# The FFN and scan stage of a decoder kernel: tile product behind a chunk's first scan, statistics and normalisation by rows, features in halves, another order of the first loads, the last state summed by TensorE

## The reference

```python
x = x + L0_ffn(layernorm(x), lut, gate_idx, up_idx, down_idx)
# gate = xn @ lut[gate_idx].T ; up = xn @ lut[up_idx].T          (1376 columns each)
# out  = (silu(gate) * up) @ lut[down_idx].T

def step(state, xs):                    # 512 channels x 16 states, 512 steps, 4 sequences
    dA = jnp.exp(d_t[..., None] * A)
    state = state * dA + (d_t * u_t)[..., None] * B_t[:, None, :]
    y_t = jnp.einsum('ben,bn->be', state, C_t)
```

## Time and profile before

| | us |
|---|---|
| median of 3 runs (lowest to highest) | 2331.14 (2330.18 to 2335.35) |
| the profiled execution's own time | 2330.81 |
| its span from first to last instruction | 2329.0 |
| PE busy | 2123.0 (91%) |
| DVE busy | 1740.6 (75%) |
| POOL busy | 1064.9 (46%) |
| ACT busy | 955.4 (41%) |

### The profile page before, as it was taken

One profiled execution on the slowest core, in us unless ns is written; L12 is line 12 of the kernel. 1 busy time (PEld: TensorE's weight loads), 2 busy tenths in 40 slices (PEclk: granted clock), 3 DMA queues, 4 the chain that ended last, 5 costly groups with the idle time before them and its releaser, 6 DMA issues. The chain is left out here.

```text
span 2329.0 us, 25406 instructions
## 1 busy us (share of the span) xinstructions
PE 2123.0 (91%) x7538; PEld 1145.1 (49%) x7538; DVE 1740.6 (75%) x2988; ACT 955.4 (41%) x1827; POOL 1064.9 (46%) x811
## 2 busy tenths in 40 slices
PE   6999999999999998996899998999699999999858
PEld 3555555455545553444646556465354545455334
DVE  3888788978888877886888888889646474665554
ACT  2433334334334335664646546466224232332321
POOL 3553433334435512233899898999631011010143
PEclk9999999999999999998999999999789999999979
DMA  7000000000000011656535526453264243432121
GB/s 272 24 19 19 19 23 23 16 26 19 18 19 23 19 49 63 225 220 243 206 135 190 194 91 207 141 202 110 82 198 118 73 116 94 108 109 69 50 113 54
DMA packets 100377, 232.73 MB, mean 100 GB/s; under 512 B 16542, under 2 KB 33824, under 8 KB 97844
## 3 DMA queue, kind: packets, MB, share of 16 engines
q1 hardware_dynamic: 86504, 183.71, 24.4%
q10 hardware_dynamic: 13260, 47.73, 6.0%
q0 software_dynamic: 512, 0.13, 0.0%
HBM read 158.89 MB, written 46.27 MB: 88 GB/s over the span
## 5 line engine op out<-in xcount | busy, mean ns | idle before, releaser
L1583 POOL TENSOR_TENSOR s_state<-s_b_rows,s_delta_u 128x1024 f32<-128x1024 f32 x128 | 303.4, 2383 | 37.6 <-DMA s_b_rows<-scan_bc 35.2
L1627 DVE TENSOR_TENSOR_SCAN s_state<-s_decay,s_state 128x512 f32<-128x512 f32 x256 | 305.0, 1212 | 13.5 <-ACT s_decay L1569 11.0
L908 POOL TENSOR_SCALAR a_prob<-a_prob,a_rsum 128x256 f32<-128x256 f32 x256 | 143.4, 579 | 373.1 <-DVE a_rsum L781 373.0
L1742 PE MATMUL c_bank<-c_xn_parts,c_w_parts 128*128 128x512 f32 (+1 forms) x1056 | 275.8, 412 | 6.5 <-DMA c_w_parts<-ffn_weights_lo 6.4
L1569 ACT ACTIVATE s_decay<-s_delta,s_a 128x512 f32<-128x512 f32 x256 | 173.5, 689 | 229.3 <-DVE s_state L1627 223.5
L1742 PEld LDWEIGHTS c_bank<-c_xn_parts,c_w_parts 128*128 128x128 f32 (+1 forms) x1056 | 201.0, 191 | 68.7 <-issue 21.0
L433 DVE TENSOR_SCALAR f_picks<-f_mask,f_lut_xor,f_lut 128x260 int32<-128x260 int32 x512 | 228.5, 519 | 7.6 <-DVE f_mask L424 0.6
L580 PE MATMUL a_bank<-a_xn_t,a_wq_then_context 128*128 128x512 f32 x512 | 224.3, 592 | 0.0
L641 PE MATMUL a_bank<-a_wo,a_out_t 128*128 128x512 f32 x512 | 222.3, 592 | 0.0
L2257 ACT ACTIVATE d_prob_t<-d_score 128x512 f32<-128x512 f32 x256 | 139.0, 596 | 175.0 <-PE d_score L2124 174.1
L443 DVE COPY_PREDICATED f_picks<-f_mask,f_picks 128x260 int32<-128x260 int32 x448 | 193.6, 491 | 21.1
(11 more groups left out here) (224 smaller groups left out, 3738.0 us busy)
## 6 DMA issues: line engine op xcount, KB each, us to landing
s_b_rows<-scan_bc SPq DMA_DIRECT2D x64, 512.0 KB, 3.8
c_w_parts<-ffn_weights_hi ACTq DMA_DIRECT2D x39, 512.0 KB, 3.7
c_w_parts<-ffn_weights_lo ACTq DMA_DIRECT2D x39, 512.0 KB, 4.9
d_unit<-diff_parts SPq DMA_DIRECT2D x26, 512.0 KB, 3.8
f_idx<-in_idx SPq DMA_DIRECT2D x64, 130.0 KB, 2.2
ffn_weights<-f_picks SPq DMA_DIRECT2D x64, 130.0 KB, 1.7
d_qs<-d_hi SPq DMA_DIRECT2D x128, 64.0 KB, 2.0
d_factor<-in_factors SPq DMA_DIRECT2D x16, 512.0 KB, 3.6
```

Source lines behind the costliest of these rows:

```text
L1583: pool.tensor_tensor(self.state[:, s], row.broadcast_to([P, 2, T]), self.delta_u[:, h % 2], ALU.mult) \
L1627: dve.tensor_tensor_scan(self.state[:, s, e, :], self.decay[u % 2][:], self.state[:, s, e, :], 0.0, ALU.mult, ALU.add).then_inc(self.scann ...
L1742: mm = nc.tensor.matmul(banks[b][0:width[o], :], w_parts[:, n % SLOTS, w, at:at + width[o]], xn_parts[:, x_, k, :], start=((k, w, x_) == t ...
```

## The change

- `lift` and the statistics and normalisation of the next pass move behind the first scan of the chunk and ahead of the weighing (`beside`). The statistics are made one row tile at a time at pieces 4 to 7, their moments at piece 8, and the normalised rows are written one at a time at pieces 12 to 15.
- The features at piece 28 are taken in two halves, two ahead of the chunk's second scan and two behind it.
- At the start of the stage ACT loads weight tile 0 (before: tile 1), and SP loads weight tile 1 behind the first pair of B rows (before: tile 0, ahead of delta, delta_u and the rows).
- At the end the last chunk is weighed ahead of the last `add`, POOL no longer adds it to its group, and PE adds it to y itself; DVE takes each half of y as soon as it is ready.

```diff
--- before.py
+++ after.py
@@ -1465,6 +1465,7 @@
         self.weighed = core.sem("s_weighed")
         self.gathered = core.sem("s_gathered")
         self.summed = core.sem("s_summed")
+        self.last_summed = core.sem("s_last_summed")
         self.y_taken = core.sem("s_y_taken")
 
     def sync_setup(self, sp):
@@ -1500,11 +1501,13 @@
         sp.dma_start(self.scratch["y"][h // 2, :, h % 2 * 2:h % 2 * 2 + 2, :], self.y[:]) \
             .then_inc(self.stored, 16)
 
-    def sync(self, sp):
+    def sync(self, sp, behind_first_row):
         self.load_half(sp, 0)
         for h in range(2 * B):
             for r in range(8 * h, 8 * h + 8):
                 self.load_rows(sp, r)
+                if r == 0:
+                    behind_first_row()
                 if r == 8 * h + 4:
                     if h:
                         self.store_half(sp, h - 1)
@@ -1536,6 +1539,17 @@
                                        start=(g % 4 == 0), stop=(g % 4 == 3))
         mm.then_inc(self.summed, 1)
 
+    def sum_last(self, pe):
+        g, c = self.GROUPS - 1, self.N - 1
+        pe.wait_ge(self.gathered, 3 * g + 2)
+        for e in range(2):
+            self.nc.tensor.matmul(self.y_bank[e][:], self.consts.ident[:], self.group[:, g % 2, e, :],
+                                  start=False, stop=False)
+        pe.wait_ge(self.weighed, c + 1)
+        for e in range(2):
+            self.nc.tensor.matmul(self.y_bank[e][:], self.consts.ident[:], self.state[:, c % self.SLOTS, e, :],
+                                  start=False, stop=True).then_inc(self.last_summed, 1)
+
     def tensor_setup(self, pe):
         self.spread_c(pe, 0)
 
@@ -1546,7 +1560,7 @@
             self.sum_group(pe, (c - 6) // 4)
 
     def tensor_end(self, pe):
-        self.sum_group(pe, self.GROUPS - 1)
+        self.sum_last(pe)
 
     def scalar_setup(self, act):
         act.wait_ge(self.a_in, 16)
@@ -1607,8 +1621,7 @@
             self.feed(pool, c + 2)
 
     def gpsimd_end(self, pool):
-        for c in (self.N - 2, self.N - 1):
-            self.gather(pool, c)
+        self.gather(pool, self.N - 2)
 
     def vector_setup(self, dve):
         dve.wait_ge(self.a_step, 1)
@@ -1637,15 +1650,20 @@
 
     def take_y(self, dve, h):
         dve.wait_ge(self.y_in, (h + 1) * 16)
-        dve.wait_ge(self.summed, 4 * h + 4)
+        if h < 2 * B - 1:
+            dve.wait_ge(self.summed, 4 * h + 4)
         for e in range(2):
+            if h == 2 * B - 1:
+                dve.wait_ge(self.last_summed, e + 1)
             dve.tensor_tensor(self.y[:, e, :], self.y_bank[e][:], self.y[:, e, :], ALU.add) \
                 .then_inc(self.y_taken, 1)
 
-    def vector(self, dve, c):
+    def vector(self, dve, c, behind_scan, behind_weighing):
         self.scan(dve, c, 0)
+        behind_scan()
         if c:
             self.weigh(dve, c - 1)
+        behind_weighing()
         self.scan(dve, c, 1)
         if c % 16 == 3 and c > 16:
             self.take_y(dve, c // 16 - 1)
@@ -1708,8 +1726,7 @@
         @block.sync
         def _(sp):
             scan.sync_setup(sp)
-            load_weights(sp, 0, 0)
-            scan.sync(sp)
+            scan.sync(sp, lambda: load_weights(sp, 0, 1))
             scan.sync_end(sp)
 
         @block.tensor
@@ -1793,7 +1810,7 @@
                         act.wait_ge(full[1], fill_turn(i, o) + 1)
                     load_weights(act, *divmod(n, OT))
 
-            load_ahead(1)
+            load_ahead(0)
             features(0)
             scan.scalar_setup(act)
             for n in range(2, SLOTS):
@@ -1814,8 +1831,8 @@
 
         @block.vector
         def _(dve):
-            def features(i):
-                for k in range(KD):
+            def features(i, tiles=range(KD)):
+                for k in tiles:
                     dve.wait_ge(xn_rounded, i * KD + k + 1)
                     nc.vector.tensor_tensor(xn_parts[:, 1, k, :], banks[k % 2][:], xn_parts[:, 0, k, :].bitcast(F32),
                                             ALU.subtract).then_inc(free[k % 2], 1)
@@ -1830,6 +1847,39 @@
                 dve.wait_ge(full[tt % 2], down_turn(i, tt) + 1)
                 nc.vector.tensor_tensor(x[:, i, tt, :], banks[tt % 2][:], x[:, i, tt, :], ALU.add) \
                     .then_inc(free[tt % 2], 1)
+
+            def stats_row(i, tt):
+                row = nc.vector.bn_stats(norm.stats[:, tt, :], x[:, i, tt, :])
+                if tt == TT - 1:
+                    row.then_inc(norm.stats_done, 1)
+
+            def moments(i):
+                wait_apart(dve, norm.stats_done, i * 2 + 1, norm.waited)
+                for tt in range(TT):
+                    last = nc.vector.bn_aggr(norm.mean_var[:, tt, :], norm.stats[:, tt, :])
+                last.then_inc(norm.stats_done, 1)
+                dve.wait_ge(norm.stats_done, i * 2 + 2)
+                nc.vector.tensor_scalar(norm.var_eps[:], norm.mean_var[:, :, 1], EPS, None, ALU.add) \
+                    .then_inc(norm.var_ready, 1)
+
+            def apply_row(i, tt):
+                dve.wait_ge(norm.rstd_ready, i + 1)
+                nc.vector.tensor_scalar(norm.xn[tt], x[:, i, tt, :], norm.mean_var[:, tt, 0:1],
+                                        norm.rstd[:, tt:tt + 1], ALU.subtract, ALU.mult).then_inc(norm.xn_ready, 1)
+
+            def beside(i, j):
+                if 2 <= j <= FILLS and j % 2 == 0:
+                    lift(i, j // 2 - 1)
+                if i + 1 < B and 0 <= j - (STATS_AT - TT) < TT:
+                    stats_row(i + 1, j - (STATS_AT - TT))
+                if i + 1 < B and j == STATS_AT:
+                    moments(i + 1)
+                if i + 1 < B and 0 <= j - NORM_AT < TT:
+                    apply_row(i + 1, j - NORM_AT)
+
+            def half_features(i, j, n):
+                if j == XN_AT and i + 1 < B:
+                    features(i + 1, range(2 * n, 2 * n + 2))
 
             norm_skip(dve, norm, 1)
             norm_ahead(nc, norm, ahead["ffn_first"], x, 0)
@@ -1837,20 +1887,17 @@
             scan.vector_setup(dve)
             for i in range(B):
                 for j in range(PIECES):
-                    if 2 <= j <= FILLS and j % 2 == 0:
-                        lift(i, j // 2 - 1)
                     if j > FILLS and j != XN_AT + 1 and (j == XN_AT or down_piece(j)[1] == 0):
                         add(i, 1 if j == XN_AT else down_piece(j)[0] - 1)
-                    if i + 1 < B and j == STATS_AT:
-                        norm_stats(nc, dve, norm, x, i + 1)
-                    if i + 1 < B and j == NORM_AT:
-                        norm_apply(nc, dve, norm, x, i + 1)
+                    if not chunks[j]:
+                        beside(i, j)
+                        half_features(i, j, 0)
                     for c in chunks[j]:
-                        scan.vector(dve, 32 * i + c)
-                    if j == XN_AT and i + 1 < B:
-                        features(i + 1)
+                        scan.vector(dve, 32 * i + c, lambda: beside(i, j), lambda: half_features(i, j, 0))
+                    half_features(i, j, 1)
+                if i == B - 1:
+                    scan.weigh(dve, scan.N - 1)
                 add(i, TT - 1)
-            scan.weigh(dve, scan.N - 1)
             ahead["diff_first"].vector(dve, x, 0)
             scan.take_y(dve, 2 * B - 1)
 
```

## The result

The changed kernel took 2341.26 us (median of 13 runs), the kernel before 2332.05 in the same job: ratio 1.0036 with a 95% interval of 1.0022 to 1.0049, 5 to 11 us slower. Both say slower; only the size differs. The prediction had it 4 us faster.

A forecast was written before the change was run, and what follows sets the result against it. A ring of waits between ACT's decays and DVE bounds the kernel. Start -0.4, passes 0 and 1 -0.5 each, pass 2 -0.3, pass 3 +3.35, clock -1.5, tail -4.3: together -4.1, median 2327.0 us, range 2324.5 to 2329.5.

The forecast's parts named there:

- Ring (price): Scan pieces: product inside DVE's half of the ACT-DVE ring makes two chunks take 8.76 us, before 8.14; pass 3 +2.7.
- +0.65: From chunk 18 to the first addition: PE's last wait, for the weighing behind the product, costs 0.65 us in every pass.
- A normalised row costs 0.48: Passes 0 to 2: a normalised row costs DVE 0.48 us at an even piece, nothing at an odd one.
- Features: Features of the next pass: two ahead of the second scan start 1.13 us earlier; passes 0 to 2 gain 1.15 each.
- Clock, "-1.5": PE behind the features: shorter idle saves nothing or 1.5 us in each of passes 0 and 1; -1.5 taken.
- Start, "-0.4": Stage start: B rows earlier on SP's queue, with a half share of DMA engines, bring the third scan 0.4 us earlier.
- the best case: Stage start: B rows moved from seventh to fifth on SP's queue land 2.5 us earlier; ruled out by the rule of turns.
- the other side: Stage start: ACT's earlier transfers delay the second pair of B rows behind the down weights, +4.7 us; called the likelier side.
- Tail, -4.3: Stage end: the last weighing no longer waits and PE adds the last chunk, so y is taken 4.3 us earlier.
- C: Rival, stage start: B rows land behind the down weights and the clock keeps falling; +2.5 us, 2333.6; chance 0.13.
- E: Rival: ACT's rounding comes too late for earlier features and the start stays; +1.2 us, 2332.3; chance 0.16.
- D: Rival: DVE's even piece stays at 3.38, about 28 products of 0.62 cost nothing; -17 more, 2309.7; chance 0.06.

The follow-up runs named there:

- the version with lumps: Changed kernel with statistics and normalisation back in lumps at pieces 8 and 12 ahead of the first scan; ratio 1.0015, stage 607.4 us.
- the kernel with the other form of row: Changed kernel with normalised rows made by scalar_tensor_tensor in place of tensor_scalar, at the same places; ratio 1.0047, stage 611.1 us.
- part 2: Parts taken out of the changed kernel; with the tile product back ahead of the first scan, stage 589.2 us instead of 607.0, ratio 0.9960.
- behind a third: Kernel before with only the tile product moved behind the chunk's first scan, statistics and normalisation staying in lumps; ratio 1.0060, stage 614.6 us.

## Why the prediction was wrong

The profiled execution took 2340.40 where the sum gave 2326.7, 13.7 more: 6.7 in the stage, 3.8 behind it and 2.9 ahead of it. In the stage the normalised rows and the clock were priced too low, while the start gave more than it was given; the code behind the stage was left out of the sum; the ring was right.

- **Ring (price): right.** 8.74 to 8.76 for two pieces, 19.03, 30.75 and 35.73 against 19.13, 30.83 and 35.64, and 40.0 us of waits for the decay in 36 places (predicted some 25), 19 of them of 1.31. Pass 3 lost 2.4 instead of 3.35. The three steps from chunk 18 on did cost 0.8, as "+0.65" says, but chunk 28's step came out 1.2 shorter (6.74, before 7.93), so the stretch is 54.3 where it was 54.7. What the prediction didn't see is that this price ate more than the gains it listed: with start, tail and halves in, the same move costs 18 to 19.
- **"A normalised row costs 0.48" (the step that failed).** The price came from a lump laid where POOL happened to be idle. Spread out, one of four in a pass met the whole of a product of POOL and took 2.42, its piece 6.33 instead of 4.48: +1.85 in each of passes 0 to 2. The sum of variance and epsilon met another, 0.95 to 0.99: the moments' step 5.27 instead of 4.78, +0.5 a pass. Together +7, against the forecast and not against the lumps: the version with lumps has the same stage (607.4), so the long rows took what spreading them should have given.
- **Features: right,** 1.1 in each pass, idle 2.18 against 2.17.
- **Clock, "-1.5": the bounds were too narrow.** The steps gave 1.6 in pass 1, took 1.5 in pass 2 (addition of piece 32: wait 1.38 before, 2.91 after) and 1.3 at piece 25 of pass 1, where PE's granted clock was 0.51 from 1327.1 to 1330.5: +1.2 in sum where -1.5 was forecast. The last was named as what would make the forecast wrong, and given no price.
- **Start, "-0.4": mis-sized,** -2.8, a little more than the best case. Counted from the stage's start, the two pairs of rows landed at 13.7 and 19.8, where the prediction had 15.1 and 22.6. The second held POOL up by 1.34 only. From the rule of turns between queues (the Trainium skill, DMA: Bandwidth & Descriptors, section Queues, rings and completion order) the prediction had taken the other side to be the likelier; the run went against that reading, and doesn't show the turns themselves.
- **Tail, -4.3: right,** -4.5.
- **Missing: the code behind the stage, +3.8,** taken as unchanged because its text is. The same 2578 matmuls keep PE busy 582.02 there instead of 578.93, and 82 us instead of 71 stand at 1.2 GHz. How the stage ahead brings that about was not tried and stays open: the kernel with the other form of row had the longer stage and only 68 us at half clock behind it.

In numbers, stage of the prediction -4.1, measured +2.6: start -2.4, passes 0 to 2 by +2.7, +2.2 and +4.0, pass 3 by -1.0, tail -0.2, the clock term of 1.5 that lies in the passes; sum +6.8, which is the 6.7 but for rounding.

None of the rivals was it. C (slower, queue starved) had the sign and the size of the stage, by luck: its mechanism, rows that land late, didn't come. E (+1.2) had the sign, and its mechanism, features that gain nothing, didn't come either. D is refuted by the steps of 3.98 and 4.76; its size, 17 for 28 products, is close to the 18 and 19 that the product costs in part 2, of which some 2 to 3 go with the clock.

## What to carry to other kernels

Before work is moved into a wait, ask who ends the next wait: here it was ACT, with two table loads between decays that it could make only as far ahead as two banks allow. A third decay bank, at the price of one of the two C banks, took 32 us off the changed stage (607.0 to 574.5). Cost a VectorE operation with POOL running, not from a place where POOL idles: copies, tensor_scalar and operations on two tensors in SBUF took up to about a whole POOL instruction more here. Statistics rows, and operations on two tensors of which one lay in PSUM, did not. And try the parts of a change one at a time and together, for two parts can win the same wait: three of this one's gave 12 us together (0.9948), and the product behind the scan took more than all of it.

## What was not expected of the hardware

An operation on four elements in a partition took 2.18 us, since it waited out POOL's product; the exclusion holds the other way too, POOL's product 2.78 instead of 2.35 to 2.40 behind an addition of 0.68. And identical code behind the stage ran 652.2 and 652.3 us long with 71 us at half clock behind one kernel's stage, and 656.0 twice with 82 behind the other's; behind a third it ran 661.8 with 95, in a single profile.
